# Attention output kept transposed and normalised through DMAs, row maxima turned in a score bank, negated maxima made by GpSimd

## What is computed

```python
Q, K, V = (xn @ W + b, split into 16 heads of 16)
scores = einsum('bqhd,bkhd->bhqk', Q, K) * scale + alibi
attn = softmax(scores, axis=-1)
out = einsum('bhqk,bkhd->bqhd', attn, V).reshape(B, S, D)
x = x + (out @ Wo + bo) + moe(xn) + shared_expert(xn)
```

## Time and profile before

| | us |
|---|---|
| median of 3 runs | 2854.55 (2844.99 to 2878.88) |
| the profiled execution | 2862.6 |
| its span, first to last instruction | 2860.8 |
| PE / DVE / ACT / POOL busy in the span | 92% / 74% / 59% / 27% |
| projections, and the first maxima | 0 to about 235 |
| attention | about 235 to 1854 |
| expert blocks | 1855 to 2340 |
| shared stage | 2340 to 2861 |

### The profile page before, as it was taken

One profiled execution on the slowest core, in us unless ns is written; L12 is line 12 of the kernel. 1 busy time (PEld: TensorE's weight loads), 2 busy tenths in 40 slices (PEclk: granted clock), 3 DMA queues, 4 the chain that ended last, 5 costly groups with the idle time before them and its releaser, 6 DMA issues. The chain is left out here.

```text
span 2860.8 us, 43410 instructions
## 1 busy us (share of the span) xinstructions
PE 2641.9 (92%) x16474; PEld 1636.4 (57%) x16474; DVE 2120.8 (74%) x3582; ACT 1696.7 (59%) x2442; POOL 772.4 (27%) x792
## 2 busy tenths in 40 slices
PE   5998999999999998888888999899999999999998
PEld 4774333333333333333333333399999998888887
DVE  7977888888888887676777888477777775445444
ACT  2445666677677776565656777777777773223222
POOL 4333431000000004233332000143333434334433
PEclk9998999999999999898989999999999999999999
DMA  6986553112111113233232111177777763223322
GB/s 203 346 290 192 183 163 95 43 36 58 43 51 51 36 51 105 80 98 102 80 105 61 36 52 39 66 241 239 243 234 243 240 222 106 93 89 115 107 89 74
DMA packets 190447, 357.43 MB, mean 125 GB/s; under 512 B 26448, under 2 KB 132112, under 8 KB 180880
## 3 DMA queue, kind: packets, MB, share of 16 engines
q1 hardware_dynamic: 152128, 192.03, 21.6%
q0 software_dynamic: 37024, 161.83, 17.7%
q10 hardware_dynamic: 1088, 0.79, 0.1%
HBM read 232.07 MB, written 132.51 MB: 127 GB/s over the span
## 5 line engine op out<-in xcount | busy, mean ns | idle before, releaser
L947 DVE TENSOR_REDUCE mx<-ps 128x1 f32<-128x512 f32 x2048 | 1282.5, 684 | 261.1 <-PE ps L472 203.0
L472 PE MATMUL ps<-OPS 54*128 54x512 f32 (+1 forms) x4096 | 947.1, 456 | 135.1 <-DVE mx L947 80.3
L472 PEld LDWEIGHTS ps<-OPS 54*128 54x128 f32 (+1 forms) x4096 | 477.2, 194 | 871.3 <-DVE mx L947 314.3
L796 ACT ACTIVATE pta<-ps 128x1024 f32<-128x1024 f32 x512 | 503.5, 1022 | 247.0 <-PE ps L472 231.0
L796 ACT ACTIVATE ptb<-ps 128x1024 f32<-128x1024 f32 x512 | 499.1, 1022 | 239.2 <-PE ps L472 183.0
L472 PE MATMUL ps<-OPS,WB 128*128 128x256 f32 (+1 forms) x2268 | 367.6, 313 | 3.1 <-DVE WB L1071 1.6
L1214 POOL TENSOR_TENSOR ot<-accs,rc 128x128 f32<-128x128 f32 x128 | 49.4, 406 | 1165.1 <-DVE rc L958 1165.1
L472 PEld LDWEIGHTS ps<-OPS,WB 128*128 128x128 f32 x2268 | 309.6, 180 | 30.8 <-issue 3.5
L472 PE MATMUL ps<-ptb,VB 128*32 128x512 f32 x2048 | 292.1, 645 | 0.0
L472 PE MATMUL ps<-pta,VB 128*32 128x512 f32 x2048 | 284.2, 628 | 0.0
L472 PE MATMUL ps<-OPS,WB0c 128*128 128x256 f32 (+3 forms) x1440 | 256.1, 329 | 2.0 <-ACT accs L803 1.1
(11 more groups left out here) (158 smaller groups left out, 2932.3 us busy)
## 6 DMA issues: line engine op xcount, KB each, us to landing
OPS<-QKh SPq DMA_DIRECT2D x512, 64.0 KB
Xs<-zero POOLq DMA_DIRECT2D x71, 256.0 KB, 4.0
xr<-Xs SPq DMA_DIRECT2D x71, 256.0 KB
Ys<-VB SPq DMA_DIRECT2D x71, 256.0 KB
QKh<-qkH SPq DMA_DIRECT2D x16, 1024.0 KB, 6.1
QKl<-qkL SPq DMA_DIRECT2D x16, 1024.0 KB, 8.0
OPS<-QKl SPq DMA_DIRECT2D x256, 64.0 KB
xt<-in_x SPq DMA_DIRECT2D x16, 512.0 KB, 5.9
```

The costliest lines, as they stand in the source:

```text
L472: return self.e.matmul(o, l, r, start=start, stop=stop)
L796: self.e.activation(pt(n), ps[:, b:b + 2, :], ACT.Exp).then_inc(sem["exp"], 1)
L947: e.reduce_max(mx[:, k2, hh, i, half:half + 1], ps[:, bank, :], AX.X).then_inc(sem["mxred"], 1)
```

## The change

1. `heads` becomes four steps with an index i, called at the end of the kc = 0, 2, 4 and 6 attention with i = kc/2, for pair r-1. The turns on PE, the copy L807, the reciprocal of 128x16 on DVE, and the two products on POOL go. Instead: (0) SP waits for `acc1` and copies the four rows of sums to `sq` with four DMAs, each one row of 512 numbers to 32 partitions of 16; (1) DVE takes the reciprocal of `sq` (128x16), and SP writes it to DRAM (`Sd`); (2) SP waits for that and reads it back with four DMAs, each row broadcast to 16 partitions, into `asum`; (3) POOL multiplies `accs` by `asum` (128x512), SP waits for it and stores with four DMAs to `OTd`, which has the head dimension as rows.
2. The shared stage loads its columns from `OTd` directly; the eight transposes of a group go, and ACT and DVE read SBUF instead of PSUM.
3. `max_rows` turns into bank 0, a score bank, instead of the ring: it waits for an exponential, stands after the eighth u of the kc=4 attention instead of the sixth, and the next scores into bank 0 wait for `mrev`. The ring has only the u's (and two routing products).
4. The negated maxima are made by POOL with three operations of 128x16 (negate, round, remainder); ACT's L778 and DVE's L952 go.

The calls, cut to the core:

```diff
     def attention(self, s, n):
         r, kc = divmod(s, 8)
         if s % 2 == 0:
...
-                    if u == MAXU and kc == 4 and r + 1 < NPAIR:
-                        self.max_rows(r + 1)
-                    if u == NU and kc == 2 and r >= 1:
-                        self.heads(r - 1)
-                else:
+                else:
+                    if v == 1 and kc == 4 and r + 1 < NPAIR:
+                        self.max_rows(r + 1)
                     if s >= 2:
                         self.values(*divmod(s - 2 + v, 8))
                     v += 1
+            if r >= 1:
+                self.heads(r - 1, kc // 2)
         if kc == 0 and r >= 1 and r + 2 < NPAIR:
             for i in range(4):
                 self.load_pair(r + 2, i)
```

TensorE:

```diff
             def max_rows(self, r, bank=None):
...
-                    bank = self.ring_bank("rows", r)
+                    bank = 0
+                    self.w.wait_ge("exp", 16 * (r - 1) + 11)
...
             def scores(self, r, kc, hh, half):
...
                 self.w.wait_ge("exp", n - 1)
+                if kc == 6 and half == 0:
+                    self.w.wait_ge("mrev", min(r + 2, NPAIR))
...
-            def heads(self, r):
-                self.w.wait_ge("acc1", r + 1)
-                bank = self.ring_bank("heads", r)
-                for c in range(4):
-                    q = self.turn(ps[:, bank, c * P:(c + 1) * P], accs[:, r % 2, c * P:(c + 1) * P])
-                q.then_inc(sem["ht"], 1)
...
-            def o_columns(self, g):
```

VectorE, and GpSimd:

```diff
                     e.tensor_reduce(m16[:, k2, :, :], mx[:, k2, :, :, :], AX.X, ALU.max).then_inc(sem["m16"], 1)
-                    self.w.wait_ge("mnh", r + 1)
-                    e.scalar_tensor_tensor(mneg[:, k2, :, 1, :], m16[:, k2, :, :], -1.0, mneg[:, k2, :, 0, :],
-                                           ALU.mult, ALU.subtract).then_inc(sem["mnl"], 1)
...
+            def heads(self, r, i):
+                if i == 1:
+                    self.w.wait_ge("asd", 64 * (r + 1))
+                    self.e.reciprocal(sq[:, :], sq[:, :]).then_inc(sem["rcp"], 1)
...
+            def max_unit(self, n, bank=None):
...
+                    self.w.wait_ge("m16", r + 1)
+                    e.tensor_scalar(m16[:, k2, :, :], m16[:, k2, :, :], -1.0, None, ALU.mult).then_inc(sem["mng"], 1)
...
+                    e.tensor_copy(mneg[:, k2, :, 0, :].bitcast(F32R), m16[:, k2, :, :]).then_inc(sem["mnh"], 1)
...
+                    e.tensor_tensor(mneg[:, k2, :, 1, :], m16[:, k2, :, :], mneg[:, k2, :, 0, :], ALU.subtract
+                                    ).then_inc(sem["mnl"], 1)
...
+            def heads(self, r, i):
+                if i != 3:
+                    return
+                self.w.wait_ge("asb", 64 * (r + 1))
+                self.e.tensor_tensor(accs[:, r % 2, :], accs[:, r % 2, :], asum[:, :], ALU.mult
+                                     ).then_inc(sem["nrm"], 1)
```

SyncE:

```diff
+                if i == 0:
+                    self.w.wait_ge("sdw", 16 * r)
+                    self.w.wait_ge("acc1", r + 1)
+                    for q in range(4):
+                        e.dma_start(sq[32 * q:32 * q + 32, :], accs[32 * q + HD:32 * q + HD + 1, k, :]
+                                    ).then_inc(sem["asd"], 16)
+                elif i == 1:
+                    self.w.wait_ge("asb", 64 * (r - 1))
+                    self.w.wait_ge("rcp", r + 1)
+                    e.dma_start(Sd[k].rearrange("(p n) -> p n", p=P), sq[:, :]).then_inc(sem["sdw"], 16)
+                elif i == 2:
...
+                    self.w.wait_ge("sdw", 16 * (r + 1))
+                    for q in range(4):
+                        e.dma_start(asum[32 * q:32 * q + HD, :],
+                                    Sd[k, q * GT:(q + 1) * GT].rearrange("(a n) -> a n", a=1).broadcast_to([HD, GT])
+                                    ).then_inc(sem["asb"], 16)
+                else:
+                    self.w.wait_ge("nrm", r + 1)
+                    for q in range(4):
...
+                        e.dma_start(OTd[h0:h0 + HD, n0:n0 + GT], accs[32 * q:32 * q + HD, k, :]
+                                    ).then_inc(sem[f"ox{k}"], 16)
...
             def load_o(self, g):
...
-                self.e.dma_start(orow, od_v[g]).then_inc(sem["oro"], 16)
+                self.e.dma_start(orow[:, :, :], otd_v[:, :, g * GT:(g + 1) * GT]).then_inc(sem["oro"], 16)
```

More of the change, by code:

```diff
@@ L50 @@
     "c_ident c_bor c_w1 c_w c_ali c_r x0 x1 x2 x3 xn0 xn1 xn2 qh0 qh1 ql0 ql1 vs0 vs1 op0 op1 op2 mx0 mx1 "
[L51 to L59, removed]
+    "vst asd sdw asb ox0 ox1 zero wd xg0 xg1 sc0 sc1 wb0 wb1 wb2 xs0 xs1 xs2 xs3 yr0 yr1 xr0 xr1 oro ga0 ga1 ga2 ga3 res "
+    "xt qkmm vmm mxmm mrt smm pv rtmm sct gmm up down sdn "
+    "wsplh woh xh qkh vev mrev exp acc1 rte wsh sch sg hh yev och "
+    "wspll bq wol st ag ve norm xl qkl mxred m16 rcp rt rtm rtd rtw rts rtp rtc wslv scl hf hl ocl s1 gf fin "
+    "nhalf rstd lgc vad pad vcp ones zmem mng mnh mnl nrm wslp xb ya"
 ).split()
@@ L149, in run @@
         self.block_up(0, 0)
-        self.heads(NPAIR - 1)
+        self.heads(NPAIR - 1, 1)
         self.split_block(1, 0)
@@ L157, in run @@
             self.block_up(b, 1)
+            if b == 0:
+                self.heads(NPAIR - 1, 2)
             if b:
@@ L162, in run @@
             self.block_up(b, 2)
+            if b == 0:
+                self.heads(NPAIR - 1, 3)
             if b + 3 <= NBLK + 1:
@@ L259, in values, with heads @@
     def values(self, r, kc): pass
-    def heads(self, r): pass
+    def heads(self, r, i): pass
     def pack_expert(self, e): pass
@@ L291, in max_unit @@
             self.turns.append(("max", n))
-    def max_rows(self, r, bank=None):
-        if bank is None:
-            self.turns.append(("rows", r))
-    def heads(self, r):
-        self.turns.append(("heads", r))
     def route(self, i):
@@ L394, in build @@
         WB0 = sbuf(B, "WB0", [P, 2 * RAW], F32R)
-        ot = sbuf(B, "ot", [P, 8, D])
+        accs = sbuf(B, "accs", [P, 2, GT])
+        asum = sbuf(B, "asum", [P, GT])
+        sq = sbuf(B, "sq", [P, HD])
+        sbuf(B, "spare", [P, 2 * S - 3 * GT - HD])
         ptb = sbuf(B, "ptb", [P, NPT // 2, S])
-        accs = sbuf(B, "accs", [P, 2, GT])
-        rc = sbuf(B, "rc", [P, 2, 4, 4])
         zero = sbuf(B, "zero", [P, D])
@@ L414, in build @@
         OH, OL = (sbuf(C, n, [P, 2, GT], F32R) for n in ("OH", "OL"))
-        sbuf(C, "spare", [P, 2048])
+        sbuf(C, "sparec", [P, 2048])
         WR = [sbuf(C, f"WR{i}c", [P, RAW]) for i in range(3)]
@@ L460, in attention_over @@
         def attention_over(w):
-            w.wait_ge("od", 16 * NB)
+            for k in range(2):
+                w.wait_ge(f"ox{k}", 64 * NPAIR // 2)
             w.wait_ge("acc1", NPAIR)
-            w.wait_ge("oth", 2 * NPAIR)
             w.wait_ge("vcp", 2 * NB)
@@ L771, in project_v @@
                 self.e.copy(vs[:, k, j, :], ps[:, bank, 0:D + NE]).then_inc(sem["vev"], 1)
-            def max_unit(self, n, bank=None):
-                r, u = divmod(n, 32)
-                if u == 31:
-                    self.w.wait_ge("m16", r + 1)
-                    self.w.wait_ge("mrt", r - 1)
-                    self.e.activation(mneg[:, r % 2, :, 0, :].bitcast(F32R), m16[:, r % 2, :, :], ACT.Copy,
-                                      scale=-1.0).then_inc(sem["mnh"], 1)
             def max_rows(self, r, bank=None):
-                bank = ring.bank("rows", r) if bank is None else bank
+                bank = 0 if bank is None else bank
                 self.w.wait_ge(f"mx{r % 2}", 32 * (r // 2))
@@ L800, in values @@
                     projections_over(self.w)
-                    self.w.wait_ge("oth", 2 * (r - 1))
+                    self.w.wait_ge(f"ox{r % 2}", 64 * (r // 2))
                     self.w.wait_ge("pv", 8 * (r + 1))
                     self.e.copy(accs[:, r % 2, :], ps[:, 4, :]).then_inc(sem["acc1"], 1)
-            def heads(self, r):
-                self.w.wait_ge("ht", r + 1)
-                self.e.copy(accs[:, r % 2, :], ps[:, ring.bank("heads", r), :]).then_inc(sem["acc2"], 1)
             def route(self, i):
@@ L949, in max_unit @@
                     self.w.wait_ge("mxred", n + 1)
+                    self.w.wait_ge("mnl", r - 1)
                     e.tensor_reduce(m16[:, k2, :, :], mx[:, k2, :, :, :], AX.X, ALU.max).then_inc(sem["m16"], 1)
[L951 to L958 removed]
+            def heads(self, r, i):
+                if i == 1:
+                    self.w.wait_ge("asd", 64 * (r + 1))
+                    self.e.reciprocal(sq[:, :], sq[:, :]).then_inc(sem["rcp"], 1)
             def route(self, i):
```

78 lines of the change are left out of this document (28 added, 50 removed).

## The result

The changed kernel takes **3320.59 us** (3314.87 to 3326.42), the kernel before 2857.51 beside it (2844.99 to 2878.88): ratio 1.1612, 95% interval 1.1538 to 1.1686. It is slower by 463 us.

A forecast was written before the change was run, and what follows sets the result against it. PE bounds the kernel; late operand loads make pairs 30.1 us instead of 23.48. +347.9 over 61 pairs, -2.4 for two without loads and -12.6 in the shared stage give +333, so 3190 us, range 3050 to 3340.

The forecast's parts named there:

- stop of PE: At the first u of kc=4 attention, PE waits for late operand loads, 6.3 us in each pair.
- slow clock: PE's lower clock after each stop in attention: 1.5 us lost, between 0 and 3.
- landing of a load: From SP's last operand-load issue to the end of its traffic: 1.6 us, 1.1 to 2.2.
- P: The four value matmuls of an attention quarter on PE; 1.9 us expected right after the stop.
- scattering pairs: The 16 attention pairs in which GpSimd scatters: 4 us above a plain pair, 0 to 5.6, so 34.1 us each.

The follow-up runs named there:

- e1: Changed kernel with the 16 operand loads written ahead of the `acc1` wait and the copies into `sq`: 2907.53 us, ratio 1.0182; in a later run 2891.70 us, 1.0422.
- e2: Kernel before with one wait more: operand loads of pair r+2 wait for `acc1` of pair r-1; 3192.42 us, ratio 1.1172.
- e7: Changed kernel with loads first, reciprocal and `Sd` at kc=4, broadcasts and product at kc=6, stores behind the next pair's copies into `sq`: 2688.57 us, ratio 0.9685.
- e6: Changed kernel with GpSimd's slot clearing and expert packing moved from pairs 0 to 9 to pairs 20 to 29: 3279.36 us, ratio 1.1824.
- the first set: Earlier of two sets of comparisons; the kernel before took 2858.61 us beside it, and 2770 to 2776 beside the second.

## What to carry to other kernels

Where the order of a queue is written by hand, each DMA inherits every wait ahead of it: count the issues between a new wait and the next transfer that something needs, and put the urgent transfers ahead of the wait. Mending one such order may only pass the wait on to the next step of the queue, as e1 did; look at what SP stands before when it is late, and move that as well. A stop of PE is to be priced with its slow clock from many stops, not from one, and the landing of a load in the pairs in which other DMAs run as well as in quiet ones; work taken off PE brings time only if what PE waits for next isn't held up by a neighbour.

## What the runs showed of the hardware

- After 20 stops of 2.03 to 2.35 us (e2) came from one to four P of 1.93 us for 1.07; after two of 5.67 and 5.65 us one and three. The granted clock was 0.66 and 0.78 in two pairs with four and three of them, 0.89 and 0.94 in two with one, and 1.00 in one without a stop (e7). In the mean of 61 stops PE was busy 3.8 us longer for each.
- Loads on SP's queue landed 1.3 to 1.7 us after their last issue, and, in the changed kernel, 2.4 to 3.8 in exactly the pairs in which GpSimd clears slots, loads V or scatters (e6 moved the clearing, and the long landings with it).
- Three GpSimd operations on 128x16 took 0.25, 0.20 and 0.22 us in the median; a DMA from SBUF to `sq` 0.62 us of SP's time.
- One and the same DVE product took 0.69 us in the median, and 2.82 beside a GpSimd add of 128x1024.
- The scattering pairs took 29.1 us before, in the first set, and 22.2, as plain ones, in e7, in the second. Why is open.
